# Quantisation scales of a two-layer BitNet kernel: a guard column in the buffers, a rounding by two multiplications, and scales of several tiles in one operation

## The reference

```python
def act_quant(v):                       # per token, 8 bits
    s = 127 / clip(max|v|, 1e-5)
    return clip(round(v * s), -128, 127) / s
# ternary weights: clip(round(w / mean|w|), -1, 1) * mean|w|
# layer 0
z = layernorm(x + relu(x @ cw1[lang] + cb1) @ cw2[lang] + cb2) * gamma + beta
g = gelu(act_quant(z) @ W1q + b1)       # 1024 columns
x = x + act_quant(g) @ W2q + b2
# layer 1
y = x @ wl1[subject] + bias
h = silu(depthwise_conv3(act_quant(y) @ w1q) + conv_b)   # 1024 columns
x = x + act_quant(h) @ w2q
```

## Time and profile before

| | us |
|---|---|
| median of 3 runs | 297.47 (295.80 to 299.29) |
| the profiled execution | 294.7 |
| its span, first to last instruction | 292.9 |
| PE busy | 259.5 (89%) |
| POOL busy | 253.5 (87%) |
| DVE busy | 251.4 (86%) |
| ACT busy | 236.2 (81%) |

### The profile page before, as it was taken

One profiled execution on the slowest core, in us unless ns is written; L12 is line 12 of the kernel. 1 busy time (PEld: TensorE's weight loads), 2 busy tenths in 40 slices (PEclk: granted clock), 3 DMA queues, 4 the chain that ended last, 5 costly groups with the idle time before them and its releaser, 6 DMA issues.

```text
span 292.9 us, 6314 instructions
## 1 busy us (share of the span) xinstructions
PE 259.5 (89%) x1680; PEld 186.0 (63%) x1692; DVE 251.4 (86%) x613; ACT 236.2 (81%) x396; POOL 253.5 (87%) x366
## 2 busy tenths in 40 slices
PE   7649998799999999999989988999989989878785
PEld 7526665455565566656657866776877768646674
DVE  0379898778999999868989999999999999999563
ACT  2399998998886884785759979899898998989660
POOL 3379993789899899895999999999999999999871
PEclk9965999999999999999999999999999999999999
DMA  5895689976856854586412535536472535644493
GB/s 157 313 296 154 239 253 227 232 168 163 153 131 168 145 118 110 124 189 95 109 36 54 100 87 123 61 86 146 111 178 72 129 83 69 154 112 107 107 183 107
DMA packets 104870, 41.36 MB, mean 141 GB/s; under 512 B 89158, under 2 KB 102266, under 8 KB 104835
## 3 DMA queue, kind: packets, MB, share of 16 engines
q1 hardware_dynamic: 98384, 32.86, 51.1%
q10 hardware_dynamic: 6450, 8.10, 9.2%
HBM read 16.04 MB, written 4.19 MB: 69 GB/s over the span
## 4 chain that ended last, share of the span: by engine, by line
PE 37%; issue 16%; ACT 13%; POOL 12%; DVE 10%; DMA 7%; SPq 3%; ACTq 1%; DVEq 0%; POOLq 0%
PE banks L1418 10%; PE banks L1443 5%; PE banks L1466 4%; POOL r L856 3%; PE banks L1380 3%; ACT r L685 2%; ACT g L678 2%; DVE raw_all L1135 2%; PE banks L1495 2%; DMA raw_all<-in_w1a 2%; PE banks L1362 2%; ACT ry L647 2%; DMA cb<-in_cb 2%; DMA q1T<-r 2%; PE banks L1396 2%
## 5 line engine op out<-in xcount | busy, mean ns | idle before, releaser
L907 POOL TENSOR_TENSOR raw_all<-raw_all,mid 128x1024 f32<-128x1024 f32 (+1 forms) x31 | 55.4, 1789 | 0.1
L667 ACT ACTIVATE banks<-apad,taps 128x512 f32<-128x512 f32 x64 | 44.2, 699 | 5.6 <-DVE apad L1128 5.6
L1135 DVE SCALAR_TENSOR_TENSOR raw_all<-apad,taps,banks 128x512 f32<-128x512 f32 x64 | 46.9, 741 | 2.0 <-ACT banks L667 1.8
L897 POOL TENSOR_SCALAR mid<-apad,taps,convb 128x512 f32<-128x512 f32 x56 | 42.7, 769 | 3.2 <-DVE apad L1128 3.2
L1079 DVE TENSOR_REDUCE am<-g 128x1 f32<-128x1024 f32 x32 | 38.8, 1213 | 6.6 <-ACT g L626 6.4
L1128 DVE TENSOR_TENSOR apad<-banks,dqb 128x512 f32<-128x512 f32 x64 | 42.6, 683 | 0.3 <-PE banks L1443 0.2
L626 ACT ACTIVATE g<-banks,dqz 128x1024 f32<-128x1024 f32 x32 | 35.5, 1110 | 7.6 <-PE banks L1364 3.7
L856 POOL TENSOR_SCALAR r<-g,qs 128x1024 f16<-128x1024 f32 x32 | 36.0, 1124 | 4.3 <-DVE qs L1091 3.7
L1141 DVE TENSOR_REDUCE am<-g 128x1 f32<-128x1024 f32 x30 | 36.2, 1208 | 3.1 <-ACT g L678 3.1
L1443 PE MATMUL banks<-ryT,tern 128*128 128x512 f16 x128 | 35.9, 379 | 2.3 <-DVE raw_all L1135 2.1
L678 ACT ACTIVATE g<-banks 128x1024 f32<-128x1024 f32 x30 | 30.7, 1025 | 6.0 <-PE banks L1472 4.8
(11 more groups left out here) (145 smaller groups left out, 582.8 us busy)
## 6 DMA issues: line engine op xcount, KB each, us to landing
xs<-in_x ACTq DMA_DIRECT2D x7, 512.0 KB, 4.5
out_y<-xs SPq DMA_DIRECT2D x14, 256.0 KB, 2.4
x2T<-in_xT ACTq DMA_DIRECT2D x4, 512.0 KB, 4.3
wl<-in_cwl SPq DMA_DIRECT2D x8, 256.0 KB, 2.9
xT<-in_xT ACTq DMA_DIRECT2D x3, 512.0 KB, 7.5
cw<-in_cw SPq DMA_DIRECT2D x16, 64.0 KB, 3.7
raw_all<-in_w1a SPq DMA_DIRECT2D x1, 1024.0 KB, 6.4
raw_all<-in_w2a SPq DMA_DIRECT2D x1, 1024.0 KB, 7.9
```

Of the source, the lines that this page charges most:

```text
L667: act.activation(bank(BANK_U[g % 3]), apad[:, f, 2:S + 2], ACT.Copy, scale=taps[:, f, 2:3]).then_inc(p_last, 1)
L897: pool.tensor_scalar(middle(b, f), apad[:, f, 1:S + 1], taps[:, f, 1:2], convb[:, f:f + 1], ALU.mult, ALU.add).then_inc(p_mid, 1)
L907: pool.tensor_tensor(c[:, 2 * q:2 * q + n, :], c[:, 2 * q:2 * q + n, :], mid[q % 2][:, 0:n, :], ALU.add).then_inc(p_sum, 1)
L1135: dve.scalar_tensor_tensor(out=conv[b % 2][:, f, :], in0=apad[:, f, 0:S], scalar=taps[:, f, 0:1], in1=bank(BANK_U[(KH * b + f) % 3]), op0= ...
```

## The change

The guard moves into the data. The two buffers get a column 1024 that holds `QEPS` from the start, and the maximum runs over 1025 columns, so it is never below the guard. `scale1` goes: `inverse1` takes the reciprocal of the maximum itself, and the factor that `scale1` put in is put back by POOL's rounding, as a second multiplication by `QMAX * UNIT` in place of the addition of 0.0, and by new weight scales `wsu = ws / (127 * UNIT)` and `wsq = ws / 127` in the dequantisation scales. Layer 1 does the same for the tiles that POOL rounds (`by_pool`); the others keep `scale2`. `am1` and `am2` have four pairs of columns in place of single ones, so that POOL can read them later. `scale_z` and `scale_y` become one operation each on all their columns, with a constant array as second tensor.

```diff
+        wsu = sb("wsu", [P, 4])
+        wsq = sb("wsq", [P, 4])
-        g1 = [sb(f"g1_{k}", [P, H]) for k in range(2)]
-        am1 = [sb(f"am1_{k}", [P, 1]) for k in range(2)]
-        s1 = [sb(f"s1_{k}", [P, 2]) for k in range(2)]
+        g1_all = [sb(f"g1_{k}", [P, H + 1]) for k in range(2)]
+        g1 = [g1_all[k][:, 0:H] for k in range(2)]
+        am1 = [sb(f"am1_{n}", [P, 2]) for n in range(4)]
+        per_code = sb("per_code", [P, 2])
+        per_unit = sb("per_unit", [P, TB])
-        am2 = [sb(f"am2_{k}", [P, 1]) for k in range(TB)]
-        s2 = [sb(f"s2_{k}", [P, 2]) for k in range(PAIR)]
+        am2 = [sb(f"am2_{n}", [P, 2]) for n in range(4)]
+        s2 = [sb(f"s2_{k}", [P, 1]) for k in range(TB)]
+        def by_pool(b, k):
+            return k < 2 if b == B - 1 else k == 2
+        def scales2(b, k):
+            return 3 * b + k + 1 - (k > 2) if b < B - 1 else 3 * b + k - 1
...
             def round1(b, j):
-                pool.tensor_scalar(r1[j][:, :], g1[j % 2][:, :], qs1[j % 2][:, 0:1], 0.0, ALU.mult, ALU.add) \
+                pool.tensor_scalar(r1[j][:, :], g1[j % 2][:, :], qs1[j % 2][:, 0:1], QMAX * UNIT, ALU.mult, ALU.mult) \
             def scale_of_down1(b, p):
                 if b == 0:
-                    pool.wait_ge(s_wsc, 3)
-                pool.wait_ge(s_s1, tile(b, 2 * p + 1))
+                    pool.wait_ge(s_wsq, 1)
+                pool.wait_ge(s_am1, tile(b, 2 * p + 1))
-                pool.tensor_scalar(dq1[p][:, :], s1[p][:, :], ws[:, 1:2], 0.0, ALU.mult, ALU.add) \
+                pool.tensor_scalar(dq1[p][:, :], am1[2 * (b % 2) + p][:, :], wsu[:, 1:2], 0.0, ALU.mult, ALU.add) \
             def scale_of_down(b, p):
-                pool.wait_ge(p_s2, tile(b, 2 * p + 1))
-                pool.tensor_scalar(dq2[p][:, :], s2[p][:, :], ws[:, 3:4], 0.0, ALU.mult, ALU.add) \
+                if b == 0:
+                    pool.wait_ge(s_wsq, 2)
+                pool.wait_ge(p_am2, tile(b, 2 * p + 1))
+                w = wsq if wide_bits(b, 2 * p) else wsu
+                pool.tensor_scalar(dq2[p][:, :], am2[2 * (b % 2) + p][:, :], QEPS, w[:, 3:4], ALU.max, ALU.mult) \
             def round2(b, k):                                    # POOL's
-                pool.tensor_scalar(r2[k][:, :], silu_out(b, k), qs2[k][:, 0:1], 0.0, ALU.mult, ALU.add) \
+                pool.tensor_scalar(r2[k][:, :], silu_out(b, k), qs2[k][:, 0:1], QMAX * UNIT, ALU.mult, ALU.mult) \
...
             dve.memset(hT[A:A + 1, :], 1.0).then_inc(s_hone, 1)
+            dve.memset(per_code[:, :], 1.0 / QMAX)
+            dve.memset(per_unit[:, :], 1.0 / (QMAX * UNIT)).then_inc(s_per, 1)
+            for k in range(2):
+                ins = dve.memset(g1_all[k][:, H:H + 1], QEPS)
+            ins.then_inc(s_least, 1)
             def weight_scale(n):
+                if n % 2 == 1:
+                    dve.tensor_scalar(wsq[:, n:n + 1], ws[:, n:n + 1], 1.0 / QMAX, None, ALU.mult)
+                    dve.tensor_scalar(wsu[:, n:n + 1], ws[:, n:n + 1], 1.0 / (QMAX * UNIT), None, ALU.mult) \
+                        .then_inc(s_wsq, 1)
             def scale_z(b, p):
-                for k in range(2):
-                    ins = dve.tensor_scalar(sz[p][:, k:k + 1], amz[p][:, k:k + 1], QEPS,
-                                            1.0 / QMAX if b < Z0 else 1.0 / (QMAX * UNIT), ALU.max, ALU.mult)
-                ins.then_inc(s_sz, 1)
+                if b == 0:
+                    dve.wait_ge(s_per, 1)
+                dve.scalar_tensor_tensor(out=sz[p][:, :], in0=amz[p][:, :], scalar=QEPS,
+                                         in1=per_code[:, :] if b < Z0 else per_unit[:, 0:2],
+                                         op0=ALU.max, op1=ALU.mult).then_inc(s_sz, 1)
             def absmax1(b, j):
                 dve.wait_ge(s_gelu, tile(b, j))
-                dve.tensor_reduce(am1[j % 2][:, :], g1[j % 2][:, :], AX_X, ALU.max, apply_absolute_value=True) \
+                if b == 0:
+                    dve.wait_ge(s_least, 1)
+                wait(dve, s_dq1, pair(b - 2, j // 2))
+                dve.tensor_reduce(am1[2 * (b % 2) + j // 2][:, j % 2:j % 2 + 1], g1_all[j % 2][:, :], AX_X, ALU.max, apply_absolute_value=True) \
                     .then_inc(s_am1, 1)
-            def scale1(b, j):
-                dve.wait_ge(s_am1, tile(b, j))
-                wait(dve, s_dq1, pair(b - 1, j // 2))
-                dve.tensor_scalar(s1[j // 2][:, j % 2:j % 2 + 1], am1[j % 2][:, :], QEPS, 1.0 / (QMAX * UNIT), ALU.max, ALU.mult) \
-                    .then_inc(s_s1, 1)
             def inverse1(b, j):
-                dve.wait_ge(s_s1, tile(b, j))
+                dve.wait_ge(s_am1, tile(b, j))
-                dve.reciprocal(qs1[j % 2][:, :], s1[j // 2][:, j % 2:j % 2 + 1]).then_inc(s_qs1, 1)
+                dve.reciprocal(qs1[j % 2][:, :], am1[2 * (b % 2) + j // 2][:, j % 2:j % 2 + 1]).then_inc(s_qs1, 1)
             def scale_y(b):
-                for k in range(TB):
-                    ins = dve.tensor_scalar(sy[:, k:k + 1], amy[:, k:k + 1], QEPS, 1.0 / (QMAX * UNIT), ALU.max, ALU.mult)
-                ins.then_inc(p_sy, 1)
+                dve.scalar_tensor_tensor(out=sy[:, :], in0=amy[:, :], scalar=QEPS, in1=per_unit[:, :],
+                                         op0=ALU.max, op1=ALU.mult).then_inc(p_sy, 1)
```

More of the change, by code:

```diff
@@ L171, in build_program @@
         s_wsc = sem("s_wsc")
+        s_per = sem("s_per")
+        s_wsq = sem("s_wsq")
+        s_least = sem("s_least")
         s_low = sem("s_low")
@@ L1140, in absmax2 @@
                 dve.wait_ge(p_silu[k], b + 1)
-                dve.tensor_reduce(am2[k][:, :], silu_out(b, k), AX_X, ALU.max, apply_absolute_value=True) \
+                wait(dve, p_dq2, pair(b - 2, k // 2))
+                g = g1_all[k % 2][:, :] if by_pool(b, k) else silu_out(b, k)
+                dve.tensor_reduce(am2[2 * (b % 2) + k // 2][:, k % 2:k % 2 + 1], g, AX_X, ALU.max, apply_absolute_value=True) \
                     .then_inc(p_am2, 1)
@@ L1145, in scale2 @@
                 dve.wait_ge(p_am2, tile(b, k))
-                wait(dve, p_dq2, pair(b - 1, k // 2))
-                dve.tensor_scalar(s2[k // 2][:, k % 2:k % 2 + 1], am2[k][:, :], QEPS,
+                dve.tensor_scalar(s2[k][:, :], am2[2 * (b % 2) + k // 2][:, k % 2:k % 2 + 1], QEPS,
                                   1.0 / QMAX if wide_bits(b, k) else 1.0 / (QMAX * UNIT), ALU.max, ALU.mult) \
@@ L1151, in inverse2 @@
             def inverse2(b, k):
-                dve.wait_ge(p_s2, TB * b + k + 1)
+                if by_pool(b, k):
+                    dve.wait_ge(p_am2, tile(b, k))
+                else:
+                    dve.wait_ge(p_s2, scales2(b, k))
                 wait(dve, p_r2[k], b)
-                dve.reciprocal(qs2[k][:, :], s2[k // 2][:, k % 2:k % 2 + 1]).then_inc(p_qs2[k], 1)
+                s = am2[2 * (b % 2) + k // 2][:, k % 2:k % 2 + 1] if by_pool(b, k) else s2[k][:, :]
+                dve.reciprocal(qs2[k][:, :], s).then_inc(p_qs2[k], 1)
             def final2(b, k):
@@ L1212, in first @@
+                normalise(1, 1); absmax_z(1, 1); scale_z(1, 1); absmax1(0, 1); weight_scale(2)
+                inverse1(0, 1); inverse_z(1, 1); absmax1(0, 2); inverse1(0, 2); centre(2, 0)
                 normalise(2, 0); absmax_z(2, 0); add_adapted(3, 0); centre(2, 1); absmax1(0, 3); add_adapted(3, 1)
-                scale1(0, 3); scale_z(2, 0); inverse1(0, 3); inverse_z(2, 0); normalise(2, 1); absmax_z(2, 1)
-                absmax1(1, 0); weight_scale(3); scale1(1, 0); centre(3, 0); final1(0, 0); scale_z(2, 1)
@@ L1215, in first @@
-                inverse1(1, 0); normalise(3, 0); inverse_z(2, 1); absmax_z(3, 0); absmax1(1, 1); scale1(1, 1)
+                scale_z(2, 0); inverse1(0, 3); inverse_z(2, 0); normalise(2, 1); absmax_z(2, 1)
+                absmax1(1, 0); weight_scale(3); centre(3, 0); final1(0, 0); scale_z(2, 1)
+                inverse1(1, 0); normalise(3, 0); inverse_z(2, 1); absmax_z(3, 0); absmax1(1, 1)
                 add_adapted(4, 0); final1(0, 1); inverse1(1, 1); absmax1(1, 2); scale_z(3, 0); inverse_z(3, 0)
-                scale1(1, 2); centre(3, 1); inverse1(1, 2); absmax1(1, 3); pads(); scale1(1, 3)
@@ L1222, in first @@
[L1222 to L1226 removed]
+                centre(4, 1); add_adapted(5, 1); absmax_z(4, 0); inverse1(2, 2); absmax1(2, 3)
@@ L1234, in first @@
-                absmax1(5, 2); scale1(5, 2); absmax_z(7, 0); inverse1(5, 2); absmax_z(7, 1); absmax1(5, 3)
-                scale_z(7, 0); inverse_z(7, 0); scale1(5, 3); scale_z(7, 1); inverse_z(7, 1); inverse1(5, 3)
-                absmax_y(0, 0); absmax1(6, 0); final1(5, 0); scale1(6, 0); inverse1(6, 0); absmax1(6, 1); scale1(6, 1)
-                absmax_y(0, 1); scale_y(0); final1(5, 1); inverse_y(0); inverse1(6, 1); absmax1(6, 2); scale1(6, 2)
-                inverse1(6, 2); absmax1(6, 3); scale1(6, 3); inverse1(6, 3); absmax1(7, 0); scale1(7, 0)
@@ L1239, in first @@
```

(11 more changed lines are left out.)

38 lines of the change are left out of this document (15 added, 23 removed).

## The result

The changed kernel takes 299.55 us (median of 17 runs, 297.46 to 301.62) where the kernel before takes 296.81 in the same rounds: ratio 1.0087, 95% interval 1.0063 to 1.0111. It is 2.6 us slower, and the forecast was 0.9 us faster. Each ratio leaves out the runs over 1.5% above the fastest of their kernel, and in the rounds of four experiments one quick run of the kernel before (292.38 us) makes that 12 of its 23, so beside these four ratios stand those of the medians of all runs, 0.4 to 0.7% lower. The profiled execution has a span of 299.8 us against 292.9, 6.9 more.

The account below looks back on a forecast made before the run. POOL, end to end busy from 138 us, was taken to bound the kernel, DVE 0.7 us behind. 1.0 us gained from removed scales, less 0.1 for parts 2 and 4, gave 297.5 - 0.9 = 296.6 us; range 294.4 to 300.9.

Parts of the forecast that it names:

- What bounds the kernel: Opening step: POOL, last by 0.7 us at the end, sets the end; DVE comes next.
- POOL's closed stretch: POOL's instructions from about 138 us to 277.87 us, with no idle time before any; its start and instruction lengths move the end.
- 0.6 us a slot to spare: Second stage, per POOL round of 17.27 us: DVE can absorb 0.6 us; a longer wait for POOL would decide.
- POOL idle inside its stretch, then DVE was the bound: Sign of being wrong: idle POOL after about 137 us would mean DVE bounds and its gain counts in full.
- Part 1: Scales removed from DVE: about 7.5 us gained there, of which 1.0 us reaches POOL, bounds 0 to 2.0 us.
- The wait of 0.7 us for `scale1`: POOL's first-stage wait for DVE; it goes, and 0.36 us of it was counted as gain.
- Part 2: Added DVE work: memsets, small weight scales, guard column (1 ns of 1213), looser waits; 0.1 us in sum.
- Part 3: POOL's 41 roundings of 1.12 us become multiply, multiply: taken as 0, with 0.145 us or 0.87 us more each as further ends.
- Part 4: `scale_z` and `scale_y` with two SBUF tensor inputs may stop POOL: 0.1 us taken, 3.6 us at most.
- a rival at 20%: "DVE stands behind POOL": new `scale_z` or `scale_y` waits until POOL's reading instruction ends, +1.8 and +1.2 us, 299.6 us; 20%.
- the slow multiplication: Rival: multiply, multiply is slower on POOL, 37 roundings at 0.145 us more, 5.4 us, time 302.0 us; 7%.

Follow-up runs that it names:

- both costs undone: Changed kernel with `scale_z` and `scale_y` again one operation per column, and POOL's roundings and `dq2` as multiply, add 0.0: ratio 0.9947 to the kernel before.
- the runs that undo the changed form: `scale_z` and `scale_y` again per column: in the changed kernel 1.0035; with POOL's roundings and `dq2` also multiply, add 0.0, 0.9947.
- the one-operation form: `scale_z` and `scale_y` as one `tensor_scalar` over 2 or 4 columns: in the kernel before 1.0136, in the changed one 1.0149, there with `dq2` mostly without `max` 1.0064.
- gap undone: Changed kernel with POOL's roundings and `dq2` as multiply, add 0.0, factor and guard left out there: ratio 1.0003 to the kernel before.

## Why the prediction was wrong, point by point

- **What bounds the kernel**: right. POOL's closed stretch sets the end: the change costs 2.2 us in it, and 2.6 in all. That DVE is next was right too, as the 2.34 us hold showed. But it has less than 0.6 us a slot to spare: of the 2.18 us by which that `sy` was longer than the shortest, 1.91 came through to DVE's next first taps, 0.3 were absorbed. And the sign "POOL idle inside its stretch, then DVE was the bound" was misread: POOL was idle there by its own gaps.
- **Part 1, the removed scales**: the mechanism was right, 1.0 us with bounds 0 to 2.0; measured 1.6 us (0.4 to 2.7) with both costs undone. The wait of 0.7 us for `scale1` is gone in every kernel without it. The bounds were less safe than they looked, for they rest on the waits of one execution: the second profile of the same kernel has 3.7 us in place of 1.3 for the reciprocals. Also, as forecast, DVE's gain in the second stage moved nothing: the stretch is 136.45 us with it and 136.50 to 136.58 without.
- **Part 2**: the guard column is free, a maximum takes 1213 ns over 1025 columns, and took 1213 over 1024.
- **Part 3, "I take 0"**: the step that failed most. The rounding's duration was 1115 to 1118 ns, exactly as bounded, and the Trainium skill's rule of the port-bound body (GPSIMD Engine Reference, 3.1) held. The cost stood between the instructions, where no bound of the sum looked: 0.84 to 0.88%, 2.5 us, 1.8 of them in the stretch (138.22 to 136.45 us). All bounds were made from durations. The trace of before had the gap, though, for who adds start and duration; its timeline of POOL:

```profile
60.15 0.19 POOL L810 TENSOR_SCALAR nmean<-sums 128x2 f32<-128x2 f32 x1
60.42 1.90 POOL L785 TENSOR_SCALAR raw_all<-raw_all 128x2048 f32<-128x2048 f32 x1
```

  0.08 us between a mean and a clipping, both with constants. The change of `dq2` to `max, mult` had no term at all: in the steady slot it makes one gap itself and the rounding's too, and each takes 0.29 us for 0.26 before.
- **Part 4, "I take 0.1 us"**: mis-sized. It looked at POOL being stopped and gave the other way round to a rival at 20%. The hold is real: 0.52 and 0.56%, 1.6 us, by the runs that undo the changed form. For the one-operation form the partners without the hold ran on other chips; by all medians it is 0.46 and 0.55% (1.0080 to 1.0034, 1.0004 to 0.9949), the same. In the kernel before, with all its scales, it is 1.4%, 4.3 us, in the form with two inputs and 0.9 to 1.4% in the other. Whether it costs more there because DVE has more to do is open. In one slot of the stretch it costs 0 to 0.6 us, as it happens to fall. The rival's own price was +3.0 before the gain. Its "against" was a case in which POOL's instruction was short and half done.
- **The rival's time**, 299.6 us, is what was measured, 299.55, but that is luck: it came by two costs, 2.5 and 1.6 us, of which the rival named the smaller one and priced it at 3.0. By its reason alone (gap undone) it is 1.0003, 297.4.
- **The range**, 294.4 to 300.9, holds the time; the slow multiplication, 7%, didn't occur.

## What to carry to other kernels

Before two small DVE operations are joined into one, ask whether the new form takes the port that it shares with POOL: beside a POOL that never rests, four short operations of 0.147 us can cost less than one that waits 1 to 2 us. Where an engine runs end to end, an edit of a constant or an operation has two prices, duration and distance to the neighbours; take both from rows, by adding start and duration. Last, time the parts of a change one by one: here a gain of 1.6 us lay buried under two losses.

## What the runs showed of the hardware that I had not expected

- A DVE `tensor_scalar` of 2 or 4 fp32 columns from SBUF to SBUF waits for POOL (up to 1407 ns), one of 1 column doesn't (147 ns), nor does a reciprocal of 2 or 4 columns (160, 173 ns).
- A held DVE operation can wait for more than one POOL instruction: 2.34 us behind three middle taps without gaps. What decides how many was not tried.
- POOL loses 0.09 to 0.10 us, where it otherwise overlaps its next instruction by 0.02 us, ahead of a rounding by two multiplications when a mean, a variance, a clipping or a `max, mult` stood between it and the last one; it loses nothing when only taps, additions, splits and scales per partition did. With 0.0 or 1.0 as second constant the same rounding pays only right behind a clipping. Neither other values of the constants nor the pair of operations as written explains it: a mean behind a variance pays nothing. Which field of the instruction it is stays open.
- Two executions of the same kernel differ by 4.3 us at the first middle tap and by 0.1 us from there to the last one.
